# Four sequences instead of two in the body of the attention loop, on one core

## The reference

```python
qkv = (x @ w_qkv).reshape(b, s, 3, 16, 16)
q, k, v = jnp.moveaxis(qkv, 2, 0)
attn = softmax(einsum('bqhd,bkhd->bhqk', q, k) * 16 ** -0.5)
out = einsum('bhqk,bkhd->bqhd', attn, v).reshape(b, s, d)
x = layernorm(x + out @ w_proj + b_proj)
logits = x @ Wg.T                 # top 2 of 8 experts, capacity 5120
h = einsum('ecd,edf->ecf', exp_batches, W1)
h = gelu(h[..., :512]) * h[..., 512:]
exp_out = einsum('eci,eid->ecd', h, W2)
x = layernorm(x + gated_sum_of(exp_out))
```

## Time and profile before

| what | us |
|---|---|
| median of 3 timed runs | 3577.85 |
| lowest, highest | 3577.3, 3580.08 |
| the profiled execution | 3584.83 |
| its span, from the first to the last instruction | 3583.1 |
| attention loop, from about 252 to 1902 us of the span | 1650 |
| expert stage, from about 2110 to 3455 us | 1345 |

### The profile page before, as it was taken

The page is one execution under the profiler, slowest core; times in us unless marked ns, Lnnn a source line. Parts: engine busy times, 40 slices in busy tenths (PEclk is TensorE's granted clock), DMA queues, the critical chain, the costliest instruction groups (busy, mean ns, idle before and its releaser), DMA issues. The chain is left out here.

```text
span 3583.1 us, 68687 instructions
## 1 busy us (share of the span) xinstructions
PE 3343.3 (93%) x19714; PEld 2123.4 (59%) x19714; DVE 2485.9 (69%) x5865; ACT 1996.2 (56%) x3877; POOL 1157.3 (32%) x925
## 2 busy tenths in 40 slices
PE   6999999999999999999999869999999999999960
PEld 3444444444444444444444358888888888888850
DVE  5887888778888888888888555545454545454439
ACT  2776667667776767776677634444444444444420
POOL 1013122131313223131313243435343535443334
PEclk8999999999999999999999979999999999999985
DMA  3444445332333323232332234444344434442439
GB/s 100 145 151 155 151 154 164 102 96 79 96 86 86 93 80 97 79 100 74 100 82 82 69 84 65 74 65 70 56 71 62 76 50 74 69 59 46 61 67 335
DMA packets 397972, 340.78 MB, mean 95 GB/s; under 512 B 257720, under 2 KB 315456, under 8 KB 397632
## 3 DMA queue, kind: packets, MB, share of 16 engines
q1 hardware_dynamic: 334656, 252.20, 26.9%
q0 software_dynamic: 58368, 67.74, 11.1%
q10 hardware_dynamic: 4608, 16.78, 1.2%
HBM read 89.92 MB, written 152.17 MB: 68 GB/s over the span
## 5 line engine op out<-in xcount | busy, mean ns | idle before, releaser
L889 DVE TENSOR_REDUCE peak<-ps_rows 128x1 f32<-128x512 f32 x2048 | 1339.9, 678 | 335.8 <-PE ps_rows L564 331.6
L655 ACT ACTIVATE probs<-ps_cols 128x512 f32<-128x512 f32 x2048 | 1121.0, 601 | 295.3 <-PE ps_cols L574 291.0
L1098 PE MATMUL ps_hid<-x_hi,stack 128*128 128x512 f32 x2560 | 805.2, 396 | 32.5 <-DVE x_lo L1191 27.9
L574 PE MATMUL ps_cols<-stack 50*128 50x512 f32 x2048 | 802.1, 461 | 6.4 <-ACT probs L655 6.1
L564 PE MATMUL ps_rows<-stack 48*128 48x512 f32 x2048 | 769.7, 452 | 40.4 <-issue 30.4
L1068 POOL DMA_INDIRECT x<-out,token x320 | 503.9, 1575 | 800.3 <-ACT out L1154 670.1
L1197 DVE TENSOR_TENSOR hid<-ps_hid,act_in 128x512 f32<-128x512 f32 x320 | 219.0, 688 | 599.7 <-ACT act_in L1140 599.5
L1098 PEld LDWEIGHTS ps_hid<-x_hi,stack 128*128 128x128 f32 x2560 | 477.0, 189 | 142.2 <-DVE x_lo L1191 28.0
L564 PEld LDWEIGHTS ps_rows<-stack 48*128 48x128 f32 x2048 | 317.3, 188 | 405.5 <-DVE peak L889 279.3
L587 PE MATMUL ps_pv<-probs,v 128*17 128x512 f32 x4096 | 546.0, 605 | 1.2 <-ACT probs L655 1.2
L1098 PE MATMUL ps_hid<-x_lo,stack 128*128 128x512 f32 x1280 | 505.9, 395 | 0.0
(11 more groups left out here) (131 smaller groups left out, 3600.9 us busy)
## 6 DMA issues: line engine op xcount, KB each, us to landing
stack<-qk_hi SPq DMA_DIRECT2D x1024, 64.0 KB, 2.2
expert_rows<-blank SPq DMA_DIRECT2D x80, 520.0 KB, 3.8
quarters<-expert_rows SPq DMA_DIRECT2D x320, 128.0 KB, 2.7
stack<-qk_lo SPq DMA_DIRECT2D x512, 64.0 KB, 2.2
xs<-in_L_attn_x SPq DMA_DIRECT2D x32, 512.0 KB, 3.4
x<-row SPq DMA_DIRECT2D x32, 512.0 KB, 3.7
fy<-x SPq DMA_DIRECT2D x32, 512.0 KB, 5.0
out<-fz ACTq DMA_DIRECT2D x32, 512.0 KB, 5.1
```

The source lines that it names most:

```text
L574: pe.matmul(ps_cols[j % 2][:], k_stack[g][part, h, t * P:(t + 1) * P], q_stack[g][part, h, :], start=True, stop=True).then_inc(s_cols, 1)
L655: act.activation(probs[:, j % RING, :], ps_cols[j % 2][:], ACT.Exp, scale=SCALE).then_inc(s_exp, 1)
L889: dve.tensor_reduce(peak[s % 2][:, u:u + 1], ps_rows[n % ROWS][:], AX.X, ALU.max, negate=True).then_inc(s_max, 1)
L1098: last = pe.matmul(ps_hid[f % 2][:, part, :], w[c.par][k][:, cols], xx[c.odd][:, k, :], start=i == 0, stop=i == 3 * KT - 1)
```

## The change

The body of each loop now holds four sequences, two pairs, instead of two. The loop counts fours from 0, and the pair number is worked out from the counter and a constant. All three loops have an even number of pairs (4, 10 and 14), so nothing is left over. What is computed, in which order and with which waits, stays the same.

```diff
     for first, end in ((1, fills // 2), (fills // 2, n_seq // 2 - 1)):
         if first < end:
-            with engine.Fori(first, end) as pair:
-                for odd in (0, 1):
-                    body(Iteration(pair, odd, n_seq, end == fills // 2))
+            with engine.Fori(0, (end - first) // 2) as four:
+                for two in (0, 1):
+                    for odd in (0, 1):
+                        body(Iteration(four * 2 + (first + two), odd, n_seq, end == fills // 2))
```

## The result

The changed kernel takes 3555.91 us (median of 4 runs, 3552.62 to 3558.32) against 3577.57 us for the kernel before (4 runs, 3574.92 to 3580.08). The ratio is 0.9939, with a 95% interval of 0.9922 to 0.9956: 21.7 us faster. The forecast was 3551 with a range of 3542 to 3562. The profiled execution is 3558.32 us, 26.5 us under that of before.

What follows compares the result with a forecast made beforehand. PE was taken to set the attention loop's pace, stopping for its own code at jumps. Profiled 3584.8 - 27.2 = 3557.6 us; 23.5 to 27.2 off the timed median 3577.85 gave 3550.7 to 3554.4, stated as 3551, range 3542 to 3562.

Steps and rivals of the forecast that it cites:

- the ruler: Start times of one ACTIVATE per sequence in the attention loop: 60.4 us without a jump, 51.4 us for 13 edges.
- Part 1, the jumps: Attention loop on PE, DVE and ACT: 13 jumps become 6, saving 51.4 - 24.2 = 27.2 us.
- a later edge: One of the last nine jumps of the attention loop, priced at 3.3 us each.
- its spread: Clock falls at the four later remaining edges: none saves 32.0 us (3546), all four save 20.8 us (3557).
- The early edges: First four jumps of the attention loop, where SP also writes blank rows; 5.5 us each.
- Part 2, the other engines: Jumps of ACT, SP and POOL: nothing charged; SP's fetch, without the cover of its waits, would be 12.5 us.
- rival C: SP's doubled body is fetched and its stack loads come late: 14.7 us saved, 3563 us; 6 in 100.
- Parts 3 and 4, register operations and fetch in line: Loop body: new wait-value expressions and code read in line add nothing; upper bound for register operations 5.9 us per pair.
- A: Wait values cost PE's sequencer another ALU_OP each in the loop: 83 us against 27, 3634 us; 4 in 100.
- B: PE's pair code stays on chip, four sequences' code doesn't: 206 us less 27, about 3757 us; 2 in 100.
- D: DVE and ACT catch up at the edges; without them time returns inside sequences: 3571 to 3585 us; 4 in 100.
- The allowance: Profiled execution 7.0 us above the timed median; if all from the 13 edges, the saving is 23.5 us, not 27.2.

Runs made afterwards that it cites:

- experiment 4: The kernel before, still with pairs, each engine announcing its loop's closing branch to the instruction prefetch at the top of the body; ratio 0.9911.
- experiment 8: The kernel before with no attention loop, all 28 sequences written out on all engines; 3532.26 us, ratio 0.9872.
- experiment 7: The kernel before with four sequences in PE's loop body only, SP, POOL, ACT and DVE keeping two; 3569.94 us, ratio 0.9975.
- experiment 6: The kernel before with four sequences in the body for PE, ACT and DVE, SP and POOL keeping two; 3555.00 us, ratio 0.9932.
- experiment 12: The changed kernel with the four transposes of one round done twice in each sequence; ratio 0.9971 to the kernel before.
- Experiment 2: The kernel before with four sequences in the body for SP, POOL, ACT and DVE, PE keeping two; ratio 0.9996.
- experiment 10: The kernel before with four sequences per body on all engines and the closing branch announced to the prefetch; 3777.89 us, ratio 0.9915.
- experiment 5: The changed kernel itself, timed again against the kernel before; 3555.92 us, ratio 0.9939.

## Why the prediction was right, and where its size was off

**The mechanism.** The edge is a stop for code, at which PE, ACT and DVE jump together; seven of 13 go. This is shown: by the count of idle pieces and branches, by the branch that shrinks to 0.22 us, and the packets that go, when it is announced (experiment 4), and by the loop written out (experiment 8). The prediction priced the whole edge by the ruler, with all engines in it, and did not give it to PE alone. That was needed: PE's stop alone is worth 7.6 us (experiment 7), although the list of waits names no other cause of PE's idle time.

**Part 1, the jumps.** Expected to stay: 2 x 5.5 + 4 x 3.3 = 24.2 us; measured 27.6. The saving by the ruler is 51.4 - 27.6 = 23.8 us instead of 27.2. The mis-sized term is the 3.3 us of a later edge, which was 4.35. It was a mean over three edges with a fall of the clock and six without, on the supposition that this mix would stay. It did not: falls came at 6 of 6 edges in each of the profiles of the change (two) and of experiment 6, and at 7 of 13 before. Fewer than half of the stops brought the idle time to about a third, but took away only one fall. The prediction had this case at the edge of its spread, falls at all four later edges at 4.9 us each, 20.8 us saved and 3557 us; the result lies next to it, and not in the middle. Why the falls stay is open; experiment 12 was meant for it. Two simple reasons are put aside. It is not the length of the gap: a fall came behind one of 1.51 us (changed kernel, 1635.6 us) and none behind one of 2.26 (before, 1036.7 us). And PE's longer body alone doesn't do it: in experiment 7 PE has that body and six stops, and the clock fell behind two of them.

The early edges came out near their size, 5.1 for 5.5, but the reason suggested, that SP's blank writes lie there, is not borne out. These writes are still there in the changed kernel (DMA share 0.59 and 0.57), and the branch is 0.9 us shorter. What differs is the fetch itself. The packets of PE's code in the 2 us from the first branch on, in the kernel before:

```profile
q8 instruction: 2, 0.03, 11.0%
```

and in the changed kernel:

```profile
q8 instruction: 1, 0.02, 3.1%
```

Before, two packets move at once, read as a block in line and the jump's target; now one moves. Experiment 2 has both kinds with the blank writes over (the last one starts at 708.5 us): nine branches of PE, and the packets behind the one at 1546.2 us, which took 5.19 us, and behind the one at 1405.5 us, which took 3.85:

```profile
L152 PEldq COMPARE_BRANCH  x9: 3387/4496/5189, 850.1 to 1961.9; - x9
...
q8 instruction: 2, 0.03, 11.7%
...
q8 instruction: 1, 0.02, 4.3%
```

Over the nine profiles with unannounced jumps the 18 branches with two packets in their first 2 us took 4.50 to 5.55 us, the two of experiment 12 among them, and those with one took 3.30 to 4.27; a single one had none so early and took 4.62 (experiment 7, 405.1 us, its packet 2.2 us behind the branch). So what goes with a long branch is the second packet, with or without the writes. That the writes hold back the block in line at the early edges stays possible. No run varies the place of the branch in its block alone.

**Part 2, the other engines.** SP's body was fetched as feared (3.9 us), and the wait behind it covered that, as charged: experiment 6 puts rival C aside at its price of 12.5 us.

**Parts 3 and 4, register operations and fetch in line.** Nothing, as charged: the ruler reads 60.4 us inside bodies of four and in the loop written out. Rivals A, B and D all needed more than that. The kernel before fetches 9 packets per pair, so its body of 1506 matmuls and weight loads does not stay on chip. But it has the room: with the branch announced the same body is not fetched again (experiment 4), and the body of four sequences is (experiment 10). The Trainium skill ("Runtime: NRT & Kernel Launch", instruction fetch mechanics) gives PE room for 2048 instructions; the trace agrees only where the branch is announced, with no packet for the pairs and 76 for the fours. Rival B would need a pair that stays without the announcement.

**The sum.** Against the profiled executions 27.2 us were forecast and 26.5 measured, of which 23.8 in the loop. The remaining 2.7 us lie outside it, 2.5 of them in the expert stage, which was not edited and varies by as much between executions (1364.0 us in experiment 5, 1366.5 in experiment 8). That this sum came out nearer than its terms is luck. Against the timed runs the prediction allowed for the 7 us by which the profiled execution of before was longer, and gave 23.5 to 27.2; measured were 21.7, with an interval of 15.7 to 27.9 (0.9956 and 0.9922 of 3577.57). The allowance pointed the right way, but its lower end was still 1.8 us too much.

**A row read wrongly.** The prediction has the clock at 10 tenths in some slices of the first 1,900 us and at 9 in others. The earlier trace rows shows 9 in all of them but the first, and can't tell a full clock from one a little below. Nothing in the sum rests on it.

## What to carry to other kernels

Price a loop's back-edge (here the jump from the end of its body to the start) by the spacing of something that happens once per iteration, with and without the jump, and not by the idle time of the busiest engine: engines that stop for code beside it are hidden until it no longer stops, so change all of them at once. A branch that takes microseconds instead of tens of nanoseconds is waiting for its code; write out as much as the program can hold (here all 28 sequences, 45.3 us), or announce the branch, which for a body that fits (here a pair, not four sequences) took away every fetch of PE's code in the loop. Where the clock falls behind a stop, don't scale its cost with the number of stops.

## What the runs showed of the hardware that was not expected

The same kernels ran in two levels, steady within a series of runs: before at 3577.57 and at 3809 us, the loop written out at 3532.26 and at 3757.98 us. It is not one chip against another, since both levels were measured on one chip. The same program, written out, at the level of 3809: the ruler, 5 and then 11 us of a sequence (columns as in the earlier trace rows), and one wait:

```profile
L661 ACT ACTIVATE e_lead<-lead x28: 197/197/207, 259.4 to 2094.6; 128x4 f32<-128x4 f32 x28
...
1041.70:1046.70 5.00, 3.78 (x21) 1.30 (x18) 2.14 (x4) 1.45 (x3) 3.78 (x5) 0.95 0.62 207
1046.70:1057.70 11.00, 10.79 (x42) 5.09 (x42) 5.56 (x10) 5.90 (x12) 1.32 (x2) 0.56 0.13 46
...
ACT probs L655 <- remote: 70.5, 29, 4.9
```

and at the level of 3577, the same two stretches of a sequence:

```profile
1011.00:1016.00 5.00, 5.00 (x39) 2.21 (x35) 4.11 (x8) 3.77 (x9) 3.78 (x5) 1.00 0.56 184
1016.00:1027.00 11.00, 10.92 (x67) 4.89 (x65) 10.20 (x33) 8.45 (x18) 1.33 (x2) 1.00 0.44 124
```

In the slower series a sequence takes (2094.6 - 259.4) / 27 = 68.0 us. In the 5 us in which POOL scatters its rows PE is busy for 3.78 us instead of all 5, and in the 11 us behind that the clock is 0.56 instead of 1.00, so a loss of 1.2 us of PE's work is followed by a fall here too, as it is at many of the edges. ACT waits 70.5 us in the loop for releasers that the profile does not show ("remote"). What delays the engines is open.
